# Mamba-like mixer, block-sparse layer and attention on one core: the last mixer tile and the layer norm behind it in another order

## The chip, the core and the metric

One NeuronCore of one Trainium2 chip. Its engines are TensorE (PE in the profile; PEld is its weight load), VectorE (DVE), ScalarE (ACT), GpSimd (POOL) and SyncE (SP), which issues the transfers. Each engine takes its instructions in the order in which they are written; they meet through semaphores (`then_inc`, `wait_ge`). Matmul results land in PSUM, eight banks of 128 x 512 f32. The metric is the device time of one execution in microseconds, as the median of several.

## What is computed

1024 tokens (4 sequences of 256) of width 512 pass four residual layers. Cut to what matters here:

```python
x = x + mixer(layernorm(x))        # 128 heads of 64, chunks of 128 tokens
x = x + blocksparse(layernorm(x))  # the second layer norm; the change reaches to here
x = x + attention(layernorm(x))
x = x + gated_dense(layernorm(x))

# mixer, per head: decay within and between chunks
Lmat = exp(segment_sum(A*dt));  M = (C @ B.T) * Lmat
Y = M @ (x*dt) + between_chunks;  y = Y + D*x
y = y * rsqrt(mean(y*y) + eps) * norm_w * silu(gate)
out = y @ out_proj_w.T             # 8192 -> 512

# blocksparse: in each block of 32 of 1792 features, only the largest counts
inter = xf @ c1_w.T @ c2_w.T
idx = argmax(inter.reshape(.., 56, 32), -1)
h = relu(w1[idx] . xf);  out = sum(h * w2t[idx])
```

## The kernel before

Everything is kept transposed: features on the 128 partitions, tokens along the row. The mixer's 8192 inner features are 64 tiles `t` of 128 (two heads each), in 8 groups of 8. A list written out by hand for each engine is the order of the work; nothing is scheduled at run time. Products that need f32 accuracy are split into three fast ones (`split`, L583 to L585: high by high, low by high, high by low).

One slot of the mixer handles tile `t` and prepares tile `t + 1`. TensorE projects the next tile's x part into banks 0, 1 (`XB`) and its gate into banks 2, 3 (`GB`); it transposes tile `t` (`turn`, L617, into `YB`, banks 6, 7), it multiplies finished tiles by the output weights (`out_part`, 12 matmuls of 512 columns a call, into XB and then GB, added up by VectorE's `out_sum`, L1571), and it does the mixing itself (`outputs`, L637 and L641, into YB). ScalarE makes three decay tiles a slot: `fall_of(t, k, 0)` and `fall_of(t, k, 1)` (eight activations L1113, then an exponential L1117) and `exp_of` (L1124). All three lie in banks 4, 5 (`LB`), so each waits until VectorE has read the one before (`weigh`, L1563 for the first two, L1565 for the third). `turned` (L1556) takes the transposed tile, `outputs` needs it and all three `weigh`. Then VectorE forms y and z (L1631, L1635; for the last tile in halves of 512 tokens, L1655, L1658). ScalarE rounds z (`z_high`, L1135), GpSimd forms its low part (`z_low`, L439).

The last slot, t = 63, has no next tile. TensorE turns the tile and then does both output parts for tiles 60 and 61, and `outputs`.

Behind the groups stand, in this order: the root mean square of y (`f0` sums L729, `last_root` L1264, `last_inverse` L1667, spread to all partitions by L530); eight output parts of the last two tiles (`last_part(n)`, 6 matmuls each; n < 4 for the first 512 tokens, the rest for the second), each followed on VectorE by an add L1673 and a multiplication L1678 and on GpSimd by the addition to x (L481).

The second layer norm is done in two halves h of 512 tokens: `mean` (PE L523 on x), copy (ACT L1077), `mean_wide` (PE L530), `center` (DVE L1463), `square` (ACT L1081), `spread` (PE L523 on sq), `root` (ACT L1085), `inverse` (DVE L1468), `spread_wide` (PE L530), `scaled` (DVE L1472). Then comes the choice of blocks: `c1_part` (PE L747, f32 matmuls of 512 columns, four k for each half), `t1_high` (ACT L1268), `t1_sum` (DVE L1684), and a loop of 16 steps v: `in_part` (PE L759), reduce and compare (DVE L1719, L1723), `turn_part` (PE L796), `turned_part` (ACT L1288), `first_part` (PE L807), `mask_part` (ACT L1294). The step's compare is two behind the `in_part` it lets go. `first_part` writes the bank in which `c1_part` of half 1 lies, so the first of them waits for `t1_sum(1)`. Before the last step TensorE does the first hidden tile of the sparse layer (`hidden(0)`, L583 to L585). When the last mask is there, VectorE makes the first hidden activation (L1733), and TensorE is busy with the sparse layer from there on.

## Time and profile before

| | us |
|---|---|
| three runs | 2156.98, 2158.49, 2161.08 |
| median | 2158.49 |
| the profiled execution | 2162.24 |
| its span, first to last instruction | 2160.4 |
| TensorE busy | 2074.7 (96%) |
| VectorE busy | 1582.5 (73%) |
| ScalarE busy | 1439.5 (67%) |
| GpSimd busy | 759.0 (35%) |
| mean granted TensorE clock | 0.988 of full speed |

Busy time is a sum over all stages. The chain of work that ended last is 90% TensorE. The profile's picture of 40 slices shows TensorE at nine tenths or more nearly everywhere but in slices 26 to 28, the stretch from about 1430 to 1540 us. The change lies in that stretch.

### The profile page before, as it was taken

To read this page: it belongs to the slowest core of one execution; us is meant where nothing else is said; L and a number is where in the kernel's file an instruction comes from. 1 tells how busy PE (TensorE), PEld (TensorE's weight loads), DVE (VectorE), ACT (ScalarE), POOL (GpSimd) and SP (SyncE) were. 2 spreads that over 40 slices of the span, in tenths; PEclk is the share of its full clock that TensorE was granted. 3 is DMA by queue.
4 is the path that set the end of the run, shared out by engine and by line. 5 is a ranking of instruction groups with operands and counts; after the bars stand their busy time and mean duration, and the time that the engine had idled before them with its cause. 6 is when DMAs were issued, how large, how long until landed. Compare 5 with 4: busy or idle time off the path is not lost.

```text
span 2160.4 us, 33511 instructions
## 1 busy us (share of the span) xinstructions
PE 2074.7 (96%) x12936; PEld 1665.1 (77%) x12940; DVE 1582.5 (73%) x1701; ACT 1439.5 (67%) x3108; POOL 759.0 (35%) x391
## 2 busy tenths in 40 slices
PE   6899999999999999999999999986899989999998
PEld 4788888888888888888888888874677677777764
DVE  6778788778878887878887887777433357777765
ACT  4777786777777777777677677773533357777761
POOL 2244454444454345444444445433444100000001
PEclk9999999999999999999999999998999989999999
DMA  2222222221222122222222222221222010000001
GB/s 104 108 88 87 80 108 78 77 100 69 98 83 104 69 98 88 76 91 108 70 77 104 73 98 78 98 69 31 90 90 96 20 40 17 24 18 17 18 3 39
DMA packets 49341, 155.84 MB, mean 72 GB/s; under 512 B 13856, under 2 KB 20256, under 8 KB 40736
## 3 DMA queue, kind: packets, MB, share of 16 engines
q1 hardware_dynamic: 49184, 153.70, 20.5%
q8 instruction: 104, 1.70, 0.3%
q14 instruction: 53, 0.43, 0.1%
HBM read 151.06 MB, written 2.62 MB: 71 GB/s over the span
## 4 chain that ended last, share of the span: by engine, by line
PE 90%; DVE 7%; ACT 2%; issue 1%; DMA 0%; SPq 0%; DVEq 0%; ACTq 0%
PE PS L583 20%; PE PS L585 19%; PE PS L584 19%; PE PS L641 6%; PE PS L824 4%; PE PS L948 3%; PE PS L617 3%; PE PS L637 3%; PE PS L932 2%; PE PS L577 2%; PE PS L919 2%; PE PS L955 2%; PE PS L921 1%; PE PS L920 1%; DVE arena L1533 1%
## 5 line engine op out<-in xcount | busy, mean ns | idle before, releaser
L583 PE MATMUL PS<-xnh,wh 128*128 128x512 f32 x1272 | 510.3, 401 | 8.9 <-DVE xnl L1496 6.1
L585 PE MATMUL PS<-xnh,wl 128*128 128x512 f32 x1272 | 497.4, 391 | 0.0
L584 PE MATMUL PS<-xnl,wh 128*128 128x512 f32 x1272 | 496.5, 390 | 0.0
L1533 DVE SCALAR_TENSOR_TENSOR arena<-PS,arena 128x1020 f32<-128x1020 f32 (+2 forms) x240 | 305.6, 1273 | 31.2 <-ACT arena L1152 25.5
L1113 ACT ACTIVATE PS<-x,arena 128x128 f32<-128x128 f32 x1024 | 307.9, 354 | 22.6 <-DVE arena L1565 20.2
L583 PEld LDWEIGHTS PS<-xnh,wh 128*128 128x128 f32 x1272 | 239.6, 188 | 63.7 <-issue 14.7
L439 POOL TENSOR_TENSOR zl<-arena,zh 128x1024 fp32r<-128x1024 f32 x63 | 176.4, 2800 | 295.1 <-ACT zh L1135 295.1
L585 PEld LDWEIGHTS PS<-xnh,wl 128*128 128x128 f32 x1272 | 239.3, 188 | 52.1
L584 PEld LDWEIGHTS PS<-xnl,wh 128*128 128x128 f32 x1272 | 240.0, 189 | 46.1
L435 POOL TENSOR_TENSOR arena<-arena 128x1024 f32<-128x1024 f32 x63 | 152.0, 2412 | 296.7 <-ACT arena L1131 296.7
L424 POOL TENSOR_TENSOR wl<-arena,wh 128x1024 fp32r<-128x1024 f32 x72 | 174.8, 2428 | 200.3 <-ACT wh L1105 200.3
L583 PE MATMUL PS<-zh,woh 128*128 128x512 f32 x496 | 194.1, 391 | 0.0
L584 PE MATMUL PS<-zl,woh 128*128 128x512 f32 x496 | 194.1, 391 | 0.0
L585 PE MATMUL PS<-zh,wol 128*128 128x512 f32 x496 | 194.0, 391 | 0.0
L1571 DVE TENSOR_TENSOR sq<-sq,PS 128x1024 f32<-128x1024 f32 x124 | 150.7, 1220 | 43.3 <-PE PS L585 43.1
L641 PE MATMUL PS<-arena 128*64 128x128 f32 x2048 | 170.9, 277 | 4.4 <-DVE arena L1565 4.4
L1556 DVE TENSOR_TENSOR arena<-PS,arena 128x1024 f32<-128x1024 f32 x64 | 78.4, 1225 | 132.1 <-PE PS L617 132.1
L1765 DVE TENSOR_REDUCE arena<-PS 128x2 f32<-128x512 f32 x128 | 88.6, 693 | 113.4 <-PE PS L921 112.2
L1148 ACT ACTIVATE arena<-PS 128x1024 f32<-128x1024 f32 x64 | 65.7, 1027 | 148.6 <-PE PS L585 148.6
L1563 DVE TENSOR_TENSOR arena<-PS,arena 128x1024 f32<-128x1024 f32 x128 | 156.1, 1219 | 3.7 <-ACT PS L1117 1.5
L1124 ACT ACTIVATE PS<-x,arena 128x128 f32<-128x128 f32 x512 | 153.8, 357 | 2.2 <-DVE arena L1563 2.2
L641 PEld LDWEIGHTS PS<-arena 128*64 128x64 f32 x2048 | 120.6, 137 | 27.1 <-issue 27.1
(237 smaller groups left out, 4132.9 us busy)
## 6 DMA issues: line engine op xcount, KB each, us to landing
x<-decay SPq DMA_DIRECT2D x64, 1024.0 KB, 4.6
arena<-in_w_xg SPq DMA_DIRECT2D x72, 512.0 KB, 5.5
arena<-in_w_o SPq DMA_DIRECT2D x32, 512.0 KB, 3.4
arena<-in_w_f SPq DMA_DIRECT2D x28, 512.0 KB, 3.4
arena<-in_w_h SPq DMA_DIRECT2D x16, 257.0 KB
x<-in_x SPq DMA_DIRECT2D x3, 1024.0 KB, 7.4
out<-x SPq DMA_DIRECT2D x8, 256.0 KB, 2.0
x<-in_x SPq DMA_DIRECT2D x2, 512.0 KB, 4.2
```

Of the source, the lines that this page charges most:

```text
L424: nc.gpsimd.tensor_tensor(wl[:, k], w_raw, wh[:, k].bitcast(F32), ALU.subtract).then_inc(s["wlo"], 1)
L435: nc.gpsimd.tensor_tensor(sumsq, sumsq, ysq, ALU.add).then_inc(s["ssq"], 1)
L439: nc.gpsimd.tensor_tensor(zl[:, k], zt[:, k], zh[:, k].bitcast(F32), ALU.subtract).then_inc(s["zlo"], 1)
L583: mm(PS[:, bank], ah, bh, start=(n == 0), stop=False)
L584: mm(PS[:, bank], ah, bl, start=False, stop=False)
L585: last = mm(PS[:, bank], al, bh, start=False, stop=(n == len(terms) - 1))
L641: last = mm(PS[H, YB + u // 4, col(u % 4)], xdt[:, u, H], ring[:, hh, col(u)], start=(u % 2 == 0), stop=True)
L1113: last = act(PS[:, LB + u // 4, col(u % 4)], rowB[:, 2 * k + hh, col(u)], ACT.Relu, scale=-1.0, bias=aT[:, u, 2 * t + hh:2 * t + hh + 1])
L1124: last = act(PS[:, LB + b // 2, col(2 * hh + b % 2)], rowB[:, 2 * k + hh, col(2 * b + 1)], ACT.Exp, bias=fromend[:, k, b, hh:hh + 1])
L1533: ins = stt(o, pair_of(bank).rearrange("p q (b t) -> p q b t", t=SEQ)[:, :, :, :SEQ - k], w[:, 3 - k:4 - k], o, ALU.mult, ALU.add)
L1563: tt(both(ring[:, hh]), pair_of(LB), both(by[:, 0:TOK]), ALU.mult).then_inc(s["used"], 1)
L1571: tt(both(sq[:, m]), both(sq[:, m]), pair_of(bank), ALU.add).then_inc(s["oacc"], 1)
```

## The change

It has three parts. In the last mixer slot TensorE does one output part ahead of the turn, into GB, and the second decay tile is written to XB instead of LB. The other output part goes to XB when VectorE has read that decay tile. `outputs` signals after each half of the tokens, y of the first half waits for the first signal only, and `last_y`/`last_z` are two functions with `last_low` between them. Behind it, only `last_part(0)` stands ahead of the spread of the root mean square, where two stood. In the second layer norm the mean and centring of half 1 come directly behind those of half 0, the rest of half 1 before the choice of blocks rather than within its first steps, and `c1_part` of half 1 ends in step 0 rather than in step 1.

```diff
                     for hh in range(2):
                         last = mm(PS[H, YB + u // 4, col(u % 4)], xdt[:, u, H], ring[:, hh, col(u)], ...)
+                    if t == NT - 1 and u == NU // 2 - 1:
+                        last.then_inc(s["Y_ps"], 1)
                 last.then_inc(s["Y_ps"], 1)
+            def last_slot(t, k, q):
+                pe.wait_ge(s["oacc"], 2 * t - 4)
+                pe.wait_ge(s["wolo"], q + 1)
+                pe.wait_ge(s["zlo"], 2 * q + 3)
+                out_part(2 * k, GB)
+                turn(t, k)
+                pe.wait_ge(s["used"], 3 * t + 3)
+                out_part(2 * k + 1, XB)
+                outputs(t)
...
             last_part(0)
-            last_part(1)
             pe.wait_ge(s["f0_rc"], 2)
             pe.wait_ge(s["yv"], NT + 2)
...
-            for n in range(2, 7):
+            for n in range(1, 7):
                 last_part(n)
...
             mean_wide(1, 0)
-            spread(1, 0)
             pe.wait_ge(s["x1"], 2 * KD)
             mean(1, 1)
+            mean_wide(1, 1)
+            spread(1, 0)
             spread_wide(1, 0)
-            mean_wide(1, 1)
+            spread(1, 1)
             pe.wait_ge(s["f_in"], 16 * 4)
             pe.wait_ge(s["ln_xn"], 3)
-            c1_part(0, A, range(KD))
+            c1_part(0, A, range(2))
+            spread_wide(1, 1)
+            c1_part(0, A, range(2, KD))
             in_part(0)
-            spread(1, 1)
             in_part(1)
-            spread_wide(1, 1)
             pe.wait_ge(s["ln_xn"], 4)
+            c1_part(1, Y0, range(2))
...
-                if v < 2:
-                    c1_part(1, Y0, range(2 * v, 2 * v + 2))
+                if v == 0:
+                    c1_part(1, Y0, range(2, KD))
@@ ScalarE
                     if final and i == TPG - 1:
-                        fall_of(t, k, 1)
+                        fall_of(t, k, 1, XB)
+                        exp_of(t, k, freed=2)
                         squares(t - 1)
                         wo_high(NT // 2 - 1, woh_last)
-                        exp_of(t, k)
...
             mean(1, 0, 0)
+            mean(1, 1, 4)
             square(1, 0)
             root(1, 0, 0)
-            mean(1, 1, 4)
             square(1, 1)
+            root(1, 1, 4)
             t1_high(0, A)
-            root(1, 1, 4)
...
-                if v == 1:
+                if v == 0:
                     t1_high(1, Y0)
@@ VectorE
+                    if final and i == TPG - 1:
+                        weigh(t, 1, XB)
+                        turned(t)
+                        weigh(t, 2)
+                        out_sum(2 * k, GB, 2 * t - 3)
+                        out_sum(2 * k + 1, XB, 2 * t - 2)
+                        continue
...
-            for h in range(2):
-                last_y(h)
+            last_y(0)
+            last_z(0)
+            last_y(1)
             last_low(0)
+            last_z(1)
             last_inverse(0)
+            last_inverse(1)
             last_low(1)
-            last_inverse(1)
...
             center(1, 0)
+            center(1, 1)
...
             inverse(1, 0)
             scaled(1, 0)
-            center(1, 1)
+            inverse(1, 1)
+            scaled(1, 1)
             t1_sum(0, A)
...
-                if v == 1:
-                    inverse(1, 1)
-                    scaled(1, 1)
-                if v == 3:
+                if v == 2:
                     t1_sum(1, Y0)
```

How instructions stand on the engines. ScalarE in the last slot, before (L1113 and L1117 are a decay tile in LB, L1131 the squares, L1161 the output weights, L1124 `exp_of`):

```order
783 L1113 ACTIVATE PS<-x,arena 128x128 x8
784 L1117 ACTIVATE PS<-PS 128x1024
785 L1131 ACTIVATE arena<-arena 128x1024
786 L1161 ACTIVATE wh<-arena 128x1024
787 L1124 ACTIVATE PS<-x,arena 128x128 x8
788 L1174 ACT_TABLE_LOAD
```

and of the changed kernel, where the same functions have the lines L1126, L1130, L1144, L1174 and L1137:

```order
783 L1126 ACTIVATE PS<-x,arena 128x128 x8
784 L1130 ACTIVATE PS<-PS 128x1024
785 L1137 ACTIVATE PS<-x,arena 128x128 x8
786 L1144 ACTIVATE arena<-arena 128x1024
787 L1174 ACTIVATE wh<-arena 128x1024
788 L1187 ACT_TABLE_LOAD
```

`exp_of` has moved ahead of the squares and of the output weights.

VectorE in the last slot, before (L1556 `turned`, L1563 and L1565 `weigh`, L1571 `out_sum`, L1655 y and L1658 z in halves):

```order
914 L1556 TENSOR_TENSOR arena<-PS,arena 128x1024
915 L1563 TENSOR_TENSOR arena<-PS,arena 128x1024
916 L1571 TENSOR_TENSOR sq<-sq,PS 128x1024
917 L1565 TENSOR_TENSOR arena<-PS,arena 128x1024
918 L1571 TENSOR_TENSOR sq<-sq,PS 128x1024
919 L1655 SCALAR_TENSOR_TENSOR arena<-arena,PS 128x512
920 L1658 SCALAR_TENSOR_TENSOR arena<-arena 128x512
```

and of the changed kernel (`turned` L1569, `weigh` L1576 and L1578, `out_sum` L1584, y L1673, z L1678):

```order
914 L1576 TENSOR_TENSOR arena<-PS,arena 128x1024
915 L1569 TENSOR_TENSOR arena<-PS,arena 128x1024
916 L1578 TENSOR_TENSOR arena<-PS,arena 128x1024
917 L1584 TENSOR_TENSOR sq<-sq,PS 128x1024 x2
918 L1673 SCALAR_TENSOR_TENSOR arena<-arena,PS 128x512
919 L1678 SCALAR_TENSOR_TENSOR arena<-arena 128x512
```

The second `weigh` has moved ahead of `turned`, and both output sums behind the third `weigh`.

TensorE in the second layer norm and the first steps of the choice of blocks, before (L530 a spread to all partitions, L523 a sum on x or on its squares sq, L747 `c1_part`, L759 `in_part`, L796 `turn_part`):

```order
5682 L530 MATMUL PS<-arena,cst 128x128 x4
5683 L523 MATMUL PS<-sq,cst 32x128 x16
5684 L523 MATMUL PS<-x,cst 32x128 x16
5685 L530 MATMUL PS<-arena,cst 128x128 x8
5686 L747 MATMUL PS<-arena 128x512 x4
5687 L759 MATMUL PS<-zl,zh 128x448 x2
5688 L523 MATMUL PS<-sq,cst 32x128 x16
5689 L759 MATMUL PS<-zl,zh 128x448 x2
5690 L530 MATMUL PS<-arena,cst 128x128 x4
5691 L796 MATMUL PS<-identB,arena 128x128 x7
5692 L759 MATMUL PS<-zl,zh 128x448 x2
5693 L747 MATMUL PS<-arena 128x512 x2
```

and of the changed kernel (L756 is `c1_part`, L768 `in_part`, L806 `turn_part`):

```order
5682 L530 MATMUL PS<-arena,cst 128x128 x4
5683 L523 MATMUL PS<-x,cst 32x128 x16
5684 L530 MATMUL PS<-arena,cst 128x128 x4
5685 L523 MATMUL PS<-sq,cst 32x128 x16
5686 L530 MATMUL PS<-arena,cst 128x128 x4
5687 L523 MATMUL PS<-sq,cst 32x128 x16
5688 L756 MATMUL PS<-arena 128x512 x2
5689 L530 MATMUL PS<-arena,cst 128x128 x4
5690 L756 MATMUL PS<-arena 128x512 x2
5691 L768 MATMUL PS<-zl,zh 128x448 x4
5692 L756 MATMUL PS<-arena 128x512 x2
5693 L806 MATMUL PS<-identB,arena 128x128 x7
```

The mean of half 1 (on x) has moved ahead of the squares of half 0, the squares and both spreads of half 1 ahead of `in_part`, and the first half of the second `c1_part` ahead of the first `turn_part`.

## Rows read from the trace of the kernel before

**Rows 1.** Busy time by stage: us, engines' busy times, TensorE clock, DMA share, GB/s.

```profile
0.00:1431.00 1431.00, 1403.53 (x8785) 1167.16 (x8786) 1151.13 (x927) 1047.90 (x2109) 627.17 (x298) 1.00 0.25 88
1431.00:1451.00 20.00, 15.29 (x136) 12.86 (x135) 14.54 (x14) 14.63 (x33) 7.16 (x3) 0.91 0.32 107
1451.00:1468.00 17.00, 14.81 (x136) 11.19 (x136) 14.61 (x23) 3.00 (x7) 8.96 (x7) 1.00 0.00 1
1468.00:1501.00 33.00, 19.61 (x166) 11.17 (x162) 19.99 (x25) 7.86 (x9) 8.92 (x5) 0.84 0.25 50
1501.00:1529.00 28.00, 19.10 (x138) 11.51 (x141) 27.35 (x27) 26.32 (x32) 13.56 (x6) 0.94 0.07 20
...
1539.00:2160.00 621.00, 595.05 (x3548) 445.94 (x3548) 353.11 (x688) 334.48 (x915) 92.78 (x72) 0.98 0.13 39
```

**Rows 2.** Timeline, TensorE, last slot: start, duration, instruction, [idle before, releaser].

```profile
1438.66 1.94 PE L617 MATMUL PS<-cst,arena 128*128 128x128 f32 x8 [3.09 <-DVE arena L1631]
...
1446.98 0.44 PE L641 MATMUL PS<-arena 128*64 128x128 f32 x4 [0.43 <-DVE arena L1565]
```

**Rows 3.** Timeline, VectorE, last slot.

```profile
1440.71 1.23 DVE L1556 TENSOR_TENSOR arena<-PS,arena 128x1024 f32<-128x1024 f32 x1 [0.87 <-PE PS L617]
...
1445.61 1.23 DVE L1565 TENSOR_TENSOR arena<-PS,arena 128x1024 f32<-128x1024 f32 x1 [0.52 <-ACT PS L1124]
...
1449.86 0.75 DVE L1655 SCALAR_TENSOR_TENSOR arena<-arena,PS 128x512 f32<-128x512 f32 x1 [1.90 <-PE PS L641]
```

**Rows 4.** Timeline, ScalarE, last slot.

```profile
1437.36 2.42 ACT L1113 ACTIVATE PS<-x,arena 128x128 f32<-128x128 f32 x8 [1.36 <-DVE arena L1563]
...
1443.16 2.42 ACT L1124 ACTIVATE PS<-x,arena 128x128 f32<-128x128 f32 x8 [0.43 <-DVE arena L1563]
```

**Rows 5.** Timeline, GpSimd, slots of tiles 61 and 63, and the last addition to x.

```profile
1413.68 3.49 POOL L439 TENSOR_TENSOR zl<-arena,zh 128x1024 fp32r<-128x1024 f32 x1 [11.40 <-ACT zh L1135]
...
1448.12 2.37 POOL L439 TENSOR_TENSOR zl<-arena,zh 128x1024 fp32r<-128x1024 f32 x1 [1.47 <-ACT zh L1135]
...
1468.46 1.27 POOL L481 TENSOR_TENSOR x<-x,sq 128x512 f32<-128x512 f32 x1 [1.03 <-DVE sq L1678]
```

**Rows 6.** Timeline, VectorE, beside the first row of rows 5.

```profile
1416.64 1.61 DVE L1635 SCALAR_TENSOR_TENSOR arena<-arena 128x1024 f32<-128x1024 f32 x1
```

**Rows 7.** Timeline, TensorE, from the last output parts to step 1.

```profile
1453.70 0.47 PE L583 MATMUL PS<-zh,wh 128*128 128x512 f32 x1 [0.23 <-DVE zl L1663]
...
1456.59 0.73 PE L530 MATMUL PS<-arena,cst 1*128 1x128 f32 x16
...
1464.27 1.08 PE L523 MATMUL PS<-x,cst 128*32 128x128 f32 x32
...
1472.58 1.93 PE L523 MATMUL PS<-sq,cst 128*32 128x128 f32 x32 [4.36 <-ACT sq L1081]
...
1478.99 5.37 PE L747 MATMUL PS<-arena 128*128 128x512 f32 x8 [2.08 <-DVE arena L1472]
1486.00 0.65 PE L759 MATMUL PS<-zl,zh 128*128 128x448 f32 x2 [1.64 <-DVE zh L1684]
...
1497.78 1.88 PE L747 MATMUL PS<-arena 128*128 128x512 f32 x4
```

**Rows 8.** Timeline, VectorE, layer norm to step 3, and the first hidden activation.

```profile
1468.30 2.28 DVE L1463 TENSOR_TENSOR arena<-x,PS 128x2048 f32<-128x2048 f32 x1
...
1476.55 2.29 DVE L1472 TENSOR_TENSOR arena<-arena,PS 128x2048 f32<-128x2048 f32 x1 [0.62 <-PE PS L530]
...
1500.99 1.08 DVE L1719 TENSOR_REDUCE arena<-PS 128x28 f32<-128x896 f32 x1
...
1537.38 0.63 DVE L1733 SCALAR_TENSOR_TENSOR arena<-PS,arena 128x512 f32<-128x512 f32 x1
```

**Rows 9.** One line, the reduce of the loop: shortest, median, longest ns, first and last start.

```profile
L1719 DVE TENSOR_REDUCE arena<-PS x16: 1080/1082/1096, 1486.7 to 1526.6; 128x28 f32<-128x896 f32 x16
```

**Rows 10.** Timeline, ScalarE, the squares of half 0.

```profile
1470.61 1.91 ACT L1081 ACTIVATE sq<-arena 128x2048 f32<-128x2048 f32 x1 [4.92 <-DVE arena L1463]
```

More of the change, by code:

```diff
@@ L648, in group @@
                     n = None if final and i == TPG - 1 else t + 1
+                    if n is None:
+                        last_slot(t, k, PPG * g + i // 2 - 1)
+                        continue
                     outs = not (first and i < 2)
@@ L685, in group @@
                         q = PPG * g + i // 2 - 1
-                        if n is not None:
-                            pe.wait_ge(s["conv_x"], t + 2)
-                        else:
-                            pe.wait_ge(s["oacc"], 2 * t - 5)
+                        pe.wait_ge(s["conv_x"], t + 2)
                         pe.wait_ge(s["wolo"], q + 1)
@@ L692, in group @@
                         out_part(2 * k, XB)
-                        if n is not None:
-                            pe.wait_ge(s["sgd"], t + 2)
-                        else:
-                            pe.wait_ge(s["oacc"], 2 * t - 4)
+                        pe.wait_ge(s["sgd"], t + 2)
                         out_part(2 * k + 1, GB)
@@ L738, in last_part @@
                 if n < KD:
-                    pe.wait_ge(s["oacc"], 2 * (NT - 2) - (n < 2))
+                    pe.wait_ge(s["oacc"], 2 * (NT - 2))
                 else:
@@ L1105, in high, with fall_of @@
                 act(wh[:, k], w_raw, ACT.Copy).then_inc(s["whi"], 1)
-            def fall_of(t, k, hh):
+            def fall_of(t, k, hh, bank=LB):
                 if hh == 0:
                     ac.wait_ge(s[f"rows{k}"], 16 * (t // 2) + 16)
-                ac.wait_ge(s["used"], 3 * t + hh + 1)
-                L = pair_of(LB)
+                if bank == LB:
+                    ac.wait_ge(s["used"], 3 * t + hh + 1)
+                else:
+                    ac.wait_ge(s["oacc"], 2 * t - 5)
+                L = pair_of(bank)
                 for u in range(NU):
-                    last = act(PS[:, LB + u // 4, col(u % 4)], rowB[:, 2 * k + hh, col(u)], ACT.Relu, scale=-1.0,
+                    last = act(PS[:, bank + u // 4, col(u % 4)], rowB[:, 2 * k + hh, col(u)], ACT.Relu, scale=-1.0,
                                bias=aT[:, u, 2 * t + hh:2 * t + hh + 1])
@@ L1117, in fall_of, with exp_of @@
                 act(L, L, ACT.Exp, scale=-1.0).then_inc(s["exps"], 1)
-            def exp_of(t, k):
+            def exp_of(t, k, freed=3):
                 ac.wait_ge(s["fromend"], t + 1)
-                ac.wait_ge(s["used"], 3 * t + 3)
+                ac.wait_ge(s["used"], 3 * t + freed)
                 for b in range(NB):
@@ L1557, in turned, with weigh @@
                    across(dtT[:, :, bass.ds(2 * t, 2)].unsqueeze(3), (P, NU, 2, HP)), ALU.mult).then_inc(s["xdt"], 1)
-            def weigh(t, hh):
+            def weigh(t, hh, bank=LB):
                 ve.wait_ge(s["exps"], 3 * t + hh + 1)
@@ L1562, in weigh @@
                 if hh < 2:
-                    tt(both(ring[:, hh]), pair_of(LB), both(by[:, 0:TOK]), ALU.mult).then_inc(s["used"], 1)
+                    tt(both(ring[:, hh]), pair_of(bank), both(by[:, 0:TOK]), ALU.mult).then_inc(s["used"], 1)
                 else:
@@ L1589, in group @@
                         ve.wait_ge(s["gtm"], 2 * g + 2)
-                    if not (final and i == TPG - 1):
-                        weigh(t, 0)
+                    if final and i == TPG - 1:
[4 more added lines that the diff above has]
+                        out_sum(2 * k + 1, XB, 2 * t - 2)
+                        continue
+                    weigh(t, 0)
                     if side == 1:
@@ L1625, in group @@
                     ve.wait_ge(s["Y_ps"], t + 1)
-                    if final and i == TPG - 1:
-                        continue
                     if final and i == TPG - 2:
@@ L1653, in last_y, with last_z @@
             def last_y(h):
+                ve.wait_ge(s["Y_ps"], NT + h)
                 ve.wait_ge(s["sqd"], NT)
                 stt(yt[:, half(h)], xs[:, 1, half(h)], prm[:, NT - 1, 5:6], PS[:, YB + h], ALU.mult, ALU.add).then_inc(s["yv"], 1)
+            def last_z(h):
                 ve.wait_ge(s["yv"], NT + 1 + h)
```

## The prediction

> **What bounds the kernel now.** I read the time by stage first, then the timeline of each engine in the stretch that the change touches, following the releaser in brackets from engine to engine. By stage [rows 1], TensorE is busy 1403.5 of the first 1431 us and 595 of the last 621: there it is the bound, and the change leaves both alone. Between 1431 and 1539 us it is not: 15.3 of 20 us, 14.8 of 17, 19.6 of 33, 19.1 of 28. What bounds these 108 us is a chain that hops between engines, and the reader is to see it in four pieces.
>
> In the last slot TensorE stands idle 3.09 us until VectorE has formed y of tile 62 (L1631), and then runs its eight transposes in 1.94 us [rows 2]. ScalarE's second decay tile waits 1.36 us for the first `weigh`, and `exp_of` starts only at 1443.16 [rows 4]. So the third `weigh`, which releases `outputs`, starts at 1445.61 [rows 3] and `outputs` at 1446.98 [rows 2]; y starts when all of it is there, at 1449.86 [rows 3]. The first output part waits for z's low part, at 1453.70 [rows 7].
>
> From there to the last addition to x, TensorE's parts are the bound, one after another (14.8 us busy of 17). In the layer norm each step waits for the one before; `in_part(0)` starts at 1486.00 [rows 7]. In the choice of blocks VectorE needs two instructions a step: step 3's reduce starts at 1500.99 [rows 8] and the last, step 15's, at 1526.6 [rows 9], 2.13 us a step, and VectorE is busy 27.35 of 28 us [rows 1]. From `in_part(0)` to step 3 it takes 15.0 us, since half 1 of the norm and its `c1_part` stand in between.
>
> **The change, part by part.** I play the chain forward with durations of the rows and hand-over gaps of about 0.1 us as they show.
>
> *Last slot.* Tile 62's slot ends as before. The first output part needs the sums of slot 62, which are there, and fills TensorE's 3.09 us of idle time: 12 matmuls. Their pace is from rows 7: between 1457.25, the end of the spread at 1456.59 less its tail, and 1464.27 stand five parts, 7.0 us, so 1.36 to 1.4 a part of 6 and 2.7 for 12. The turn can't be earlier than 1438.66, since L1631 hasn't moved, but it follows work directly. ScalarE goes from its first exponential (the second decay tile waited 1.36 from 1436.0) straight to XB: 2.42 + 1.02 gives 1439.45, then `exp_of` 2.42 to 1441.9, which was 1443.16 + 2.42 = 1445.6: 3.7 earlier. On VectorE, z of tile 62 ends at 1439.8; behind it `weigh` to XB to 1441.0, `turned` to 1442.15, the third `weigh` to 1443.3 (1.2 each, rows 3). TensorE's second output part has to wait for the first of these, an added wait: 1441.15 to 1443.9, and `outputs` stands behind it in the queue. So `outputs` starts at 1443.9 instead of 1446.98, 3.1 us earlier. If TensorE finds itself at the low clock there, part and outputs take up to 1.7 longer.
>
> *Ahead of the output parts.* `outputs` takes 2.8 us and signals at its half, 1445.35; the two sums (2.4 from 1443.3) end at 1445.6, and y of half 0 follows: 4.3 us earlier than 1449.86. That would bring the first part to about 1449.2. But another releaser comes last now. GpSimd has three instructions to do, 2.4 us each: squares, output weights' low part, z's low part of tile 62. The first waits for ScalarE's squares, which stand behind `exp_of` now and are no earlier than before, so the third ends near 1450.1 instead of 1450.5, and the first output part can't start before it. Beside VectorE's L1635, which reads two operands from SBUF, that third instruction took 3.49 us and L1635 1.61, against 2.37 where it had little beside it [rows 5, 6]; now VectorE's z and low part of z, of the same kind, lie beside it, so I add 1.1: 1451.3. The price is between 0 (1450.2) and 1.1 with this row; I take the latter. The spread needs two inverses, done by 1451.2, and follows the first part at 1452.7 instead of 1456.59: 3.9 earlier. Behind it stand seven parts instead of six, 1.4 more: 2.5 left at the end of part 7.
>
> The Trainium skill, "GPSIMD Engine Reference", section 8, says that GpSimd shares its SBUF interfaces with VectorE, with contention for VectorE instructions that have two SBUF inputs. By that rule the earlier z slows GpSimd here; rows 5 and 6 agree with it (3.49 against 2.37). Without it the sum would be 1.1 larger.
>
> *Layer norm, half 0.* Centring starts at 1465.9 instead of 1468.30 [rows 8]: 2.4 gained. ScalarE has the mean copy of half 1 ahead of the squares of half 0 now. It waits for the last addition to x (1468.46 + 1.27 [rows 5], less 2.4: 1467.3), 1.1 of sums and 0.3 of copy: the squares start at 1468.8, where they could have started at 1468.2. Against 1470.61 [rows 10] that leaves 1.8. The squares' sum, root, inverse (behind centring of half 1 and 1.4 us of small VectorE instructions), spread and scaling keep 1.8: `scaled` at 1474.7 instead of 1476.55 [rows 8], and `c1_part` at 1477.1 instead of 1478.99 [rows 7].
>
> *c1 and the clock.* Its eight instructions took 5.37 us, where four of the next, in 1497.78's row, took 1.88: full clock would be 3.5 to 3.8, and 5.37 is the first half at half speed. The granted clock averages 0.84 in that stage [rows 1], since TensorE idles between the steps: 4.36 us ahead of 1472.58, whose row took 1.93 against 1.08 for the same shape at 1464.27. I take the same low clock for the first half, as TensorE's work ahead of it is still thin; the spread of half 1 (0.5) now stands within it. c1 is done at 1482.8 instead of 1484.36, and `in_part(0)` at 1484.4 instead of 1486.00: **1.6 gained** so far.
>
> *Steps 0 to 3.* Two steps of 2.13 on VectorE end at 1489.4. TensorE does two `in_part`s (0.9), half of `c1_part(1)` (1.8), turn and `in_part` (0.9, after compare 0 at 1487.3), and its second half (1.8): 1489.9. `t1_high` 0.6, `t1_sum` 0.75 bring 1491.4 for step 2 and 1493.5 for step 3, against 1500.99. That is 9.1 us from `in_part(0)`, instead of 15.0: **5.9 gained**, the largest term. It is VectorE's inverse and scaling of half 1 (3.2) with their waits, and `c1_part(1)` cut in two by steps 0 and 1, where its second half started only at 1497.78 [rows 7].
>
> *The loop and its end.* Twelve steps at 2.13 are the same. The first hidden activation comes 8.6 us after the last compare (1526.6 + 2.2 to 1537.38), because ScalarE's masks lag: it is busy 26.3 of 28 us [rows 1]. It now starts its masks about 2 us earlier relative to VectorE, of which VectorE's pace takes most back; I count **0.5**. Later stages move as a block.
>
> Sum: 1.6 + 5.9 + 0.5 = 8.0 us. The profiled execution of 2162.24 would be 2154.2; the median of the runs stands 3.75 below it, so 2158.49 - 8.0 = **2150.5**.
>
> **The rivals.**
> - *The clock stays full through `c1_part`.* TensorE has less idle time ahead of it. For: the mean of half 1 now lies in the long gap. Against: two gaps of over 1.5 us remain. It gives 1.6 more, 2148.9; with GpSimd's 1.1 as well, 2147.8.
> - *The clock is low for longer,* through both `c1_part`s. For: the stage averages 0.84 now. The second half of c1(0) and both of c1(1) at half speed cost 1.8 each, less 0.7 that was so before: 4.7, leaving 3.3 and 2155.2. This is no measurable change: a measurement of this kernel can tell about 0.2%, 4.3 us.
> - *ScalarE's mask queue, not VectorE, sets the loop's end.* The first mask follows `t1_sum` of half 1, which moves from about 1501.0 (the start of step 3's reduce) to 1491.4; all of it would reach the end: 9.6 gained, 2148.9. For: 26.3 of 28 us busy, and 8.6 us of tail. Against: its remaining 1.7 us of idle time and VectorE's 27.35.
> - *Slower.* TensorE's work in the last slot is now cut by new waits (1439.7 to 1441.15, and 1446.8 to 1451.3), and the clock falls for the output parts behind them, which are the bound of their stage: 8 parts of 1.36 double, 10.9, and the sums of the norm with c1 low too, 4.7 and 1.5. 8.0 - 17.1 = -9.1: 2167.6. It decides from about 16 us of bound TensorE work at half speed on. Against: the clock was 1.00 in 1451 to 1468 [rows 1], behind waits of the same kind.
>
> The Trainium skill, "TensorE: Matmul & The Clock Gate", Part 1, says that the throttled state is the default and activity releases it. The trace agrees (1.93 after 4.36 idle, 1.08 after work); by it alone both clock rivals are open, and none of the sums uses it.
>
> **Chances.** Forecast 0.60 (2150.5, own range 2149 to 2152.5), full clock 0.15, mask queue 0.08, clock low for longer 0.11, slower 0.04; 0.02 for anything else. The range leaves out the slower case and the outer ends of the clock cases: 2147.3 to 2154.8. Faster by over 0.2% (below 2154.2): 0.85; within: 0.11; slower: 0.04.
>
> **What would show it.** Right: an output part directly ahead of the turn, and the turn near 1.0 us; `outputs` near 1443.9; GpSimd as the releaser of the first output part, near 1451; `in_part(0)` near 1484.4; no inverse or scaling between steps 0 and 1; step 3's reduce near 1493.5; the first hidden activation near 1529.4. Wrong: the squares of half 0 later than 1469.5, a `c1_part` of half 1 at half speed, ScalarE unbroken from step 1 on, or a stage behind 1539 that grows.

## The result, and the profile after

| | before | after |
|---|---|---|
| median of 20 runs each, us | 2160.72 (2156.98 to 2166.81) | 2156.98 (2150.86 to 2161.24) |
| profiled execution, us | 2162.24 | 2154.79 |
| its span, us | 2160.4 | 2153.0 |

After to before is 0.9982, 95% interval 0.9974 to 0.9989: by this ratio the change gains 3.9 us (2.4 to 5.6), half of the 8.0 forecast; the two medians differ by 3.7. The time stands above the range's upper end of 2154.8. The two profiled executions differ by 7.4 us, but not all of it is the change's. That the profiled execution of after, at 2154.79, lies near the 2154.2 of the prediction is luck. The stretch in question begins with y of tile 62 on VectorE, and that instruction starts 2.75 us apart although nothing ahead of it was changed. Timeline, VectorE, of before (start, duration, instruction):

```profile
1437.24 1.27 DVE L1631 SCALAR_TENSOR_TENSOR arena<-arena,PS 128x1024 f32<-128x1024 f32 x1
```

The same view after:

```profile
1434.49 1.27 DVE L1648 SCALAR_TENSOR_TENSOR arena<-arena,PS 128x1024 f32<-128x1024 f32 x1
...
1442.96 0.75 DVE L1673 SCALAR_TENSOR_TENSOR arena<-arena,PS 128x512 f32<-128x512 f32 x1
1443.74 1.52 DVE L1678 SCALAR_TENSOR_TENSOR arena<-arena 128x512 f32<-128x512 f32 x1
...
1446.02 2.01 DVE L1683 TENSOR_TENSOR zl<-arena,zh 128x512 fp32r<-128x512 f32 x1
1447.95 0.74 DVE L1678 SCALAR_TENSOR_TENSOR arena<-arena 128x512 f32<-128x512 f32 x1
...
1450.58 0.63 DVE L1683 TENSOR_TENSOR zl<-arena,zh 128x512 fp32r<-128x512 f32 x1
...
1495.80 1.08 DVE L1740 TENSOR_REDUCE arena<-PS 128x28 f32<-128x896 f32 x1
...
1531.42 0.63 DVE L1754 SCALAR_TENSOR_TENSOR arena<-PS,arena 128x512 f32<-128x512 f32 x1
```

So I count from this instruction's start in every trace. To the first hidden activation it is 100.14 us before (1537.38 in [rows 8]) and 96.93 after: 3.2 us. The rest of the 7.4 lies outside. One profile is one execution, though: e8 below, which is after with nine matmuls more and has after's median, needs 100.31 for the same stretch in its profile. So a distance within one profile says where time went in that execution, and what a change is worth is read from the medians and ratios.

By stage after (us, busy times of TensorE, weight load, VectorE, ScalarE, GpSimd, TensorE clock, DMA share, GB/s), to hold against [rows 1]:

```profile
1431.00:1451.00 20.00, 15.65 (x152) 11.98 (x148) 18.63 (x18) 15.26 (x34) 7.50 (x3) 0.92 0.23 81
1451.00:1468.00 17.00, 14.26 (x134) 10.81 (x133) 13.08 (x18) 0.62 (x3) 12.24 (x10) 0.90 0.00 1
1468.00:1501.00 33.00, 25.32 (x158) 13.56 (x159) 22.69 (x27) 11.49 (x14) 5.64 (x2) 0.69 0.26 50
```

The third row is the one to stop at: the same 33 us, about as many TensorE instructions (158 against 166), and TensorE busy 25.3 us instead of 19.6. It has hardly more work; its granted clock fell from 0.84 to 0.69. TensorE's timeline says which instructions paid. First the last slot, where the change did as meant:

```profile
1435.91 1.06 PE L617 MATMUL PS<-cst,arena 128*128 128x128 f32 x8 [0.16 <-DVE arena L1648]
1438.40 0.50 PE L583 MATMUL PS<-zh,woh 128*128 128x512 f32 x1 [1.42 <-DVE arena L1576]
...
1441.38 0.44 PE L641 MATMUL PS<-arena 128*64 128x128 f32 x4
...
1448.29 0.77 PE L583 MATMUL PS<-zh,wh 128*128 128x512 f32 x1 [0.94 <-DVE zl L1683]
1448.85 0.63 PE L584 MATMUL PS<-zl,wh 128*128 128x512 f32 x1
...
1452.11 0.40 PE L584 MATMUL PS<-zl,wh 128*128 128x512 f32 x1
```

The turn follows work and takes 1.06 us, not 1.94 [rows 2]. The first output part (from 1448.29) ran at 0.63 us a matmul and the next at 0.40: it began at the low level of the clock. Matmuls overlap, so their starts tell the pace: 0.43 us apart at 0.63, 0.23 apart at 0.39. Then the layer norm and c1, the same view:

```profile
1463.59 0.51 PE L530 MATMUL PS<-arena,cst 1*128 1x128 f32 x8 [0.78 <-DVE sq L1693]
1465.65 1.93 PE L523 MATMUL PS<-x,cst 128*32 128x128 f32 x32 [1.56 <-POOL x L481]
1467.98 0.81 PE L530 MATMUL PS<-arena,cst 1*128 1x128 f32 x8 [0.40 <-ACT arena L1087]
1469.78 1.93 PE L523 MATMUL PS<-sq,cst 128*32 128x128 f32 x32 [0.98 <-ACT sq L1091]
1473.48 0.81 PE L530 MATMUL PS<-arena,cst 1*128 1x128 f32 x8 [1.77 <-DVE arena L1481]
...
1476.80 3.75 PE L756 MATMUL PS<-arena 128*128 128x512 f32 x4 [0.64 <-DVE arena L1485]
1480.47 0.81 PE L530 MATMUL PS<-arena,cst 1*128 1x128 f32 x8
1481.22 3.78 PE L756 MATMUL PS<-arena 128*128 128x512 f32 x4
1486.64 1.05 PE L768 MATMUL PS<-zl,zh 128*128 128x448 f32 x4 [1.64 <-DVE zh L1704]
1487.53 1.88 PE L756 MATMUL PS<-arena 128*128 128x512 f32 x4
```

Four c1 matmuls take 3.75 and 3.78 us here and 1.88 in the last row; the 32 small sums take 1.93 where the same shape took 1.08 in [rows 7]. From the sum at 1465.65 to the end of `c1_part(0)` everything runs at the low level, 1.2 GHz (the granted clock of that stretch is 0.50, in the last section). Before, the eight matmuls of `c1_part(0)` took 5.37 together [rows 7]; now 7.5.

One table holds the whole case, in us from the start of y of tile 62. "Forecast" is the prediction's times less 1437.24; e1, e2, e3 and e10 are the experiments below.

| start of | before | forecast | after | e1 | e2 | e3 | e10 |
|---|---|---|---|---|---|---|---|
| first half y | 12.62 | 8.4 | 8.47 | 8.45 | 12.07 | 8.47 | 12.39 |
| centring of half 0 | 31.06 | 28.7 | 29.68 | 31.73 | 30.53 | 29.35 | 32.44 |
| `scaled` of half 0 | 39.31 | 37.5 | 39.87 | 39.98 | 39.58 | 38.10 | 41.19 |
| `t1_sum(0)` | 47.86 | | 51.26 | 48.34 | 50.96 | 45.59 | 48.67 |
| reduce of step 3 | 63.75 | 56.3 | 61.31 | 64.10 | 63.62 | 55.64 | 58.72 |
| first hidden activation | 100.14 | 92.2 | 96.93 | 100.55 | 100.85 | 91.75 | 94.82 |

### The profile page after: what moved, and what is told of

It reads as the page before. It is cut to its first block, busy times and chain, and to the rows that moved or that the text cites. A ratio compares the mean times of both kernels' runs of the same rounds, so it can differ in the third digit from the quotient of the medians.

```text
span 2153.0 us, 33511 instructions
## 1 busy us (share of the span) xinstructions
PE 2075.0 (96%) x12936; PEld 1663.3 (77%) x12940; DVE 1584.8 (74%) x1701; ACT 1438.7 (67%) x3108; POOL 759.6 (35%) x391
## 4 chain that ended last, share of the span: by engine, by line
PE 90%; DVE 7%; ACT 1%; issue 1%; DMA 0%; POOL 0%; SPq 0%; DVEq 0%; ACTq 0%
PE PS L583 20%; PE PS L585 19%; PE PS L584 19%; PE PS L641 6%; PE PS L834 4%; PE PS L958 3%; PE PS L617 3%; PE PS L637 3%; PE PS L942 2%; PE PS L577 2%; PE PS L929 2%; PE PS L965 2%; PE PS L931 1%; PE PS L930 1%; DVE arena L1546 1%
## 5 line engine op out<-in xcount | busy, mean ns | idle before, releaser
L1126 ACT ACTIVATE PS<-x,arena 128x128 f32<-128x128 f32 x1024 | 307.9, 355 | 21.1 <-DVE arena L1578 20.1
L1584 DVE TENSOR_TENSOR sq<-sq,PS 128x1024 f32<-128x1024 f32 x124 | 150.6, 1220 | 42.2 <-PE PS L585 42.1
L1569 DVE TENSOR_TENSOR arena<-PS,arena 128x1024 f32<-128x1024 f32 x64 | 78.3, 1224 | 131.0 <-PE PS L617 131.0
L1161 ACT ACTIVATE arena<-PS 128x1024 f32<-128x1024 f32 x64 | 65.7, 1027 | 148.6 <-PE PS L585 148.6
L1576 DVE TENSOR_TENSOR arena<-PS,arena 128x1024 f32<-128x1024 f32 x128 | 156.1, 1220 | 3.7 <-ACT PS L1130 1.6
L1137 ACT ACTIVATE PS<-x,arena 128x128 f32<-128x128 f32 x512 | 153.9, 358 | 1.5 <-DVE arena L1576 1.5
```

Source lines behind the costliest of these rows:

```text
L1126: last = act(PS[:, bank + u // 4, col(u % 4)], rowB[:, 2 * k + hh, col(u)], ACT.Relu, scale=-1.0, bias=aT[:, u, 2 * t + hh:2 * t + hh + 1])
L1137: last = act(PS[:, LB + b // 2, col(2 * hh + b % 2)], rowB[:, 2 * k + hh, col(2 * b + 1)], ACT.Exp, bias=fromend[:, k, b, hh:hh + 1])
L1576: tt(both(ring[:, hh]), pair_of(bank), both(by[:, 0:TOK]), ALU.mult).then_inc(s["used"], 1)
L1584: tt(both(sq[:, m]), both(sq[:, m]), pair_of(bank), ALU.add).then_inc(s["oacc"], 1)
```

## Experiments

The theory after the result: the clock, low from the norm's sums through both halves of `c1_part(0)`, eats half of the gain. Rivals: the slot's new waits or contention between VectorE and GpSimd eat it; or the norm's new order costs its half 0 more than thought. All times are against the kernel before on the same chip, as a ratio with its 95% interval.

**e1_slot_only: the new slot, the norm as before.**

```
             mean_wide(1, 0)
+            spread(1, 0)
             pe.wait_ge(s["x1"], 2 * KD)
...
-            c1_part(0, A, range(2))
-            spread_wide(1, 1)
-            c1_part(0, A, range(2, KD))
+            c1_part(0, A, range(KD))
             in_part(0)
+            spread(1, 1)
```
(cut; the rest of TensorE's order up to step 1, and ScalarE's and VectorE's, are put back likewise)

> The last slot, the half-wise signal and the one part ahead of the spread as in the changed kernel; the layer norm and the choice of blocks as before. In the changed kernel's profile, set against y of tile 62, the first mean_wide of the norm comes 1.4 us earlier than before. Clock theory (the slot's gain is real, and TensorE's low clock in the norm and in c1_part ate the rest of the forecast): 1 to 2.5 us faster than before, ratio 0.9989 to 0.9995. Rival (the new order of the norm brings nothing, the slot is the whole gain): 3.9 us, ratio 0.9982.

Measured: 2160.88 us, 0.9998 (0.9989 to 1.0007). A miss: no gain at all from a slot whose first half y starts 4.2 us earlier. TensorE's timeline shows the output parts:

```profile
1448.80 0.47 PE L583 MATMUL PS<-zh,wh 128*128 128x512 f32 x1 [0.94 <-DVE zl L1681]
...
1451.23 1.24 PE L530 MATMUL PS<-arena,cst 1*128 1x128 f32 x16 [0.31 <-DVE arena L1685]
...
1453.84 0.63 PE L583 MATMUL PS<-zh,wh 128*128 128x512 f32 x1
```

Eleven matmuls, nearly two parts' worth, ran at 0.63 or more instead of 0.39, where the parts are the bound, and centring starts at 31.73 instead of 31.06 although the first output sum starts 1.7 earlier (16.64 against 18.38). In this execution the clock fell behind the slot's waits, the place of the slower rival. That the slot's waits are the cause isn't shown: e10 below has the old slot, and eight of its output matmuls were low too.

**e2_norm_only: the slot as before, the norm's new order.** The kernel before with the changed kernel's order in the norm and the choice of blocks, on all three engines, among it these lines:

```
-            c1_part(0, A, range(KD))
+            c1_part(0, A, range(2))
+            spread_wide(1, 1)
+            c1_part(0, A, range(2, KD))
             in_part(0)
...
             scaled(1, 0)
-            center(1, 1)
+            inverse(1, 1)
+            scaled(1, 1)
             t1_sum(0, A)
```

> The last slot and the output parts as before; the norm and c1_part in the new order. Clock theory: steps 0 to 3 are 5.9 us shorter, both halves of c1_part(0) run at half speed as in the changed kernel's profile and cost 3 to 4: 2 to 3 us faster than before, ratio 0.9986 to 0.9991. Rival (the order brings nothing): ratio 1.000. If the clock falls only because of what the new slot does ahead of it, this kernel gains more than the changed one, 5 us, ratio 0.9977.

Measured: 2157.73 us, 0.9987 (0.9978 to 0.9996): a gain of 2.8, as expected by the clock theory. Its TensorE timeline has the same slow c1:

```profile
1478.27 3.75 PE L747 MATMUL PS<-arena 128*128 128x512 f32 x4 [0.56 <-DVE arena L1474]
...
1482.69 3.78 PE L747 MATMUL PS<-arena 128*128 128x512 f32 x4
...
1489.74 3.62 PE L747 MATMUL PS<-arena 128*128 128x512 f32 x4
```

In this execution even the first half of `c1_part(1)` is slow (3.62), and the profile shows no gain left at the hidden activation (100.85). So the long low stretch comes with the norm's new order, slot or no slot: in all four profiles with that order and no fillers in the norm (after, e2, e5, e8) the halves of `c1_part(0)` took 3.75 and 3.78, in the three with the old order (before, e1, e4) 5.18 to 5.40 together. Its end moves from execution to execution.

**e3_fill: the changed kernel with matmuls that nobody reads, in TensorE's gaps.**

```
+            def fill(n, bank):
+                for _ in range(n):
+                    mm(PS[:, bank], woh[:, 0, 0:P], wol[:, 0], start=True, stop=True)
...
+            pe.wait_ge(s["oacc"], 2 * (NT - 2))
+            fill(1, E)
             for h in range(2):
...
+                fill(4, E)
...
             mean_wide(1, 0)
+            pe.wait_ge(s["ol_m"], 2 * KD)
+            fill(4, S)
...
+            pe.wait_ge(s["ln_xc"], 3)
+            fill(3, E)
             spread(1, 0)
+            fill(5, E)
             spread_wide(1, 0)
             spread(1, 1)
+            fill(2, S)
...
             c1_part(0, A, range(2, KD))
+            pe.wait_ge(s["ln_xn"], 4)
+            fill(4, S)
             in_part(0)
```

> The changed kernel, with matmuls of 512 columns whose result nothing reads, put into TensorE's waits from the last outputs to in_part(0) (1, 4 and 4 beside the f0 sums; 4, 3, 5, 2 and 4 in the norm). Clock theory: the clock stays full, both halves of c1_part(0) take 1.9 instead of 3.75 us, the three sums of the norm 1.1 instead of 1.9: 4 to 6 us faster than the changed kernel, 8 to 10 faster than before, ratio 0.9955 to 0.9965. Rival (hand-overs and ScalarE's order, not the clock, ate the gain): as the changed kernel, ratio 0.998; a filler that delays the next real matmul would show as 0.5 us slower.

Measured: 2151.82 us, 0.9961 (0.9949 to 0.9973): 8.4 us faster than before, with 27 matmuls more than the changed kernel. TensorE's timeline, norm and c1 (L735 is the filler):

```profile
1466.93 1.08 PE L523 MATMUL PS<-x,cst 128*32 128x128 f32 x32 [0.18 <-POOL x L481]
...
1470.21 1.08 PE L523 MATMUL PS<-sq,cst 128*32 128x128 f32 x32 [0.39 <-ACT sq L1106]
1471.22 1.42 PE L735 MATMUL PS<-wol,woh 128*128 128x512 f32 x5
...
1476.61 1.95 PE L763 MATMUL PS<-arena 128*128 128x512 f32 x4 [0.83 <-DVE arena L1500]
1478.49 0.50 PE L530 MATMUL PS<-arena,cst 1*128 1x128 f32 x8
1478.92 1.98 PE L763 MATMUL PS<-arena 128*128 128x512 f32 x4
```

Each row of the changed kernel's own work is here at the other level: 1.08 for 1.93, 1.95 for 3.75, 0.50 for 0.81. The first hidden activation comes at 91.75, 5.2 us earlier than after. From centring to `t1_sum(0)` it is 16.2 us here and 21.6 after; this distance is used again below.

**e7_fill_norm and e8_fill_parts: only the fillers from `mean_wide(1, 0)` on; only those beside the first output sums.** Each keeps one part of e3's edit.

> The changed kernel with the unread matmuls in the norm only (4, 3, 5, 2, 4). Clock theory with the loss in the norm and c1_part: most of the 4.5 us between the changed kernel and the filled one, ratio to before 0.996 to 0.9968. If the low clock in the output parts is half of the loss: 0.997.

> The changed kernel with the unread matmuls beside the f0 sums only (1, 4, 4). Clock theory with the loss in the norm: as the changed kernel, 0.998, the first output parts at full clock; 0.5 to 1 us better if the parts' low clock reached the end.

Measured: e7 2150.35 us, 0.9956 (0.9943 to 0.9969); e8 2156.76 us, 0.9983 (0.9974 to 0.9992). The gain is in the norm's fillers; those beside the first output sums add nothing that these runs can tell. The profiled execution of e7, at 2155.20 the slowest of its five, had 17 output matmuls at the low level and reached centring only at 32.56, but from there to `t1_sum(0)` it too took 16.2 us. The granted clock of one stretch in three kernels shows why (one row each: e3, e7, e8):

```profile
1465.00:1487.00 22.00, 18.34 (x173) 10.52 (x174) 16.85 (x21) 6.10 (x7) 8.94 (x5) 1.00 0.39 75
```

```profile
1465.00:1487.00 22.00, 17.77 (x182) 10.42 (x171) 15.67 (x21) 5.49 (x7) 11.08 (x7) 1.00 0.38 76
```

```profile
1465.00:1487.00 22.00, 16.07 (x136) 8.33 (x136) 12.74 (x17) 5.02 (x6) 8.91 (x5) 0.54 0.37 75
```

The changed kernel has 0.54 there, like e8.

**e9_fill_narrow: e3 with fillers of 32 columns instead of 512.** Same places, same added waits, same number of instructions.

```
-                    mm(PS[:, bank], woh[:, 0, 0:P], wol[:, 0], start=True, stop=True)
+                    mm(PS[:, bank, 0:32], woh[:, 0, 0:P], wol[:, 0, 0:32], start=True, stop=True)
```

> The filled kernel with the same number of unread matmuls at the same places, with the same waits, but of 32 columns instead of 512. If it is the clock that the filling holds up (work on TensorE, not the added instructions or waits): the clock falls again, both halves of c1_part(0) take 3.75 us, and the time is that of the changed kernel, ratio to before 0.998. If the gain came from the added waits or another side effect of the edit: 0.996, as with 512 columns.

Measured: 2155.55 us, 0.9984 (0.9975 to 0.9992), the changed kernel's ratio. TensorE's timeline:

```profile
1472.39 1.93 PE L523 MATMUL PS<-sq,cst 128*32 128x128 f32 x32 [0.54 <-ACT sq L1106]
...
1479.11 3.01 PE L763 MATMUL PS<-arena 128*128 128x512 f32 x4
...
1482.48 1.98 PE L763 MATMUL PS<-arena 128*128 128x512 f32 x4
```

The sums of squares and most of the first c1 half are slow, the second half is fast. By the ratios (intervals 0.9949 to 0.9973 and 0.9975 to 0.9992) what e3 gains it gains by TensorE's work, not by the waits or by the instructions being there. In this one profile narrow fillers hold the clock in part: from centring to `t1_sum(0)` it is 17.6 us, nearer to e3's 16.2 than to the 21.6 of after, and twelve output matmuls ahead of it were low.

**e10_norm_only_fill: e2 with the norm's fillers**, as in e7.

> The norm's new order on the kernel before, with the unread matmuls of 512 columns in the norm. With the changed kernel filled in the same places (0.9956) it shows what the new last slot is worth once the clock is no longer between: if the slot is worth the 1.6 us by which the first output sum comes earlier, this one has 0.9964; if the slot is worth nothing, 0.9956. Norm order alone had 0.9987, so the clock theory expects 4.5 to 5.5 us below that.

Measured: 2152.09 us, 0.9969 (0.9958 to 0.9980); c1 at 1.95 and 1.98. Against e2 (0.9987) the fillers are worth 0.0018 or 3.9 us, somewhat less than the 4.5 expected at least; on the whole change they are worth 5.6 (e7 against after). Against e7 (0.9956) the slot's share is 0.0013, 2.8 us, but the two intervals overlap. The interval holds the 0.9964 expected with a slot worth 1.6 us, and just leaves out the 0.9956 of a slot worth nothing.

**e4_before_fill: fillers in the kernel before.** If the clock alone made the difference, before would gain too.

```
+            pe.wait_ge(s["oacc"], 2 * (NT - 2))
+            fill(5, E)
             for h in range(2):
...
+                fill(3 * (1 - h), E)
...
             mean_wide(1, 0)
+            pe.wait_ge(s["ol_m"], 2 * KD)
+            fill(14, S)
             spread(1, 0)
...
             c1_part(0, A, range(KD))
+            fill(4, B)
```

> The kernel before, with such matmuls in its waits (5 and 3 beside the f0 sums, 14 ahead of the squares' sum of half 0, 4 behind c1_part(0)). Clock theory: there the low clock cost the first half of c1_part(0) 1.7 us, the sums 1.5 and the first part of c1_part(1) 0.9, of which 2 to 3 us lie on the chain: ratio 0.9986 to 0.9991. Rival: no change, 1.000.

Measured: 2158.61 us, 0.9999 (0.9991 to 1.0008): a miss, no gain. The sum of squares is fast, but c1 is not:

```profile
1470.32 1.08 PE L523 MATMUL PS<-sq,cst 128*32 128x128 f32 x32 [0.68 <-ACT sq L1091]
...
1476.42 5.40 PE L754 MATMUL PS<-arena 128*128 128x512 f32 x8 [2.82 <-DMA arena<-in_c]
...
1491.29 3.31 PE L754 MATMUL PS<-arena 128*128 128x512 f32 x4
```

The fillers stand ahead of the spread; behind them is a wait of 2.82 us (for `scaled`, which ends at 1475.74, then for a DMA), and c1 then takes the 5.40 that it took before (5.37 in [rows 7]), with the first half of `c1_part(1)` slow as well (3.31; it took 2.78 before). The kernel before was not filled where it mattered, so this run does not say what it would be worth with a full clock, and no other run does. How much of the fillers' gain the old order could have had stays open.

**e5_early_weights: the last output weights are split one slot earlier**, on ScalarE (`wo_high`) and GpSimd (`wo_low`), so that GpSimd has two instructions left behind the last slot, not three.

```
-                    if final and i == TPG - 1:
+                    if final and i == TPG - 2:
                         wo_low(NT // 2 - 1, wol_last, woh_last)
+                    if final and i == TPG - 1:
                         z_low(t - 1, 0)
```

> The changed kernel, with the last output weights rounded by ScalarE and their low part taken by GpSimd one slot earlier (GpSimd idles 17 us there), so that GpSimd's low part of z for tile 62 is done by about 3.5 us sooner and hardly lies beside VectorE's z and low part of z. Contention theory (these two took 1.52 and 2.01 us instead of 0.75 and 0.69 because GpSimd read SBUF beside them): both near their old durations, the first sum of an output part starts 14.9 instead of 16.8 us after y of tile 62, and the whole 1 to 2 us faster than the changed kernel if the clock behind it allows, ratio to before 0.997 to 0.9982. Rival (the order of half 0 and 1 on VectorE is what delays them): durations stay, ratio 0.9982.

Measured: 2155.78 us, 0.9983 (0.9973 to 0.9993), no different from after. VectorE's timeline:

```profile
1445.77 1.81 DVE L1680 SCALAR_TENSOR_TENSOR arena<-arena 128x512 f32<-128x512 f32 x1
...
1448.34 0.69 DVE L1685 TENSOR_TENSOR zl<-arena,zh 128x512 fp32r<-128x512 f32 x1
```

The low part of z, 2.01 after, is 0.69 with GpSimd idle beside it; z, 1.52 after, is 1.81, since GpSimd's z_low (1444.65 to 1447.03) now lies beside it, which I had not counted on. The first output sum starts at 15.60 instead of 16.80, where 14.9 was expected. These 1.2 us of chain aren't seen in the time: the ratios are 0.9983 and 0.9982. The slow c1 stays (3.75, 3.78).

**e6_fill_early: e3 and e5 together**, with `fill(4 - 2 * h, E)` beside the first output sums.

> The same together with the unread matmuls in TensorE's waits (2 instead of 4 behind the second f0 sum). If clock and contention are two separate losses they add: 1.5 to 2 us faster than with the unread matmuls alone (ratio 0.9961), ratio 0.995 to 0.9956. If the contention is hidden behind the GpSimd additions to x, 0.996.

Measured: 2150.09 us, 0.9953 (0.9941 to 0.9965), the lowest ratio of all: 10.2 us below before and clear of the changed kernel's interval. It isn't told apart from e3 or e7. Whether e5's 1.2 us adds to the fillers' gain stays open. In the profiles e6 is 1.1 us ahead of e3 at centring (28.27 against 29.35), but only 0.2 at the first hidden activation (91.51 against 91.75), since in e6 the clock was low again for the sum on x of half 1 (1.54) and the squares' sum of half 0 (1.94), although full-width fillers stood beside them.

## Why the prediction was wrong, step by step

The forecast played the chain forward, and most links came out as written. One did not, TensorE's clock, and by the start of `in_part(0)` it had cost 5 us.

*The slot.* Right in the profile. `outputs` starts 6.89 after y of tile 62, before 9.74 [rows 2]: 2.85 earlier where 3.1 stood. The first half y starts at 8.47; 8.4 stood. No part of the change failed to do what it says.

*The first output part.* Right in time by luck, wrong in cause. It starts at 13.80 (14.06 forecast). I named GpSimd as last releaser, its third instruction stretched by 1.1; the row says `DVE zl L1683`. GpSimd's z_low went only from 2.37 [rows 5] to 2.81, and ended at 1447.48. It was VectorE that paid: 1.52 for z, which takes 0.74 at 1447.95 with GpSimd done, and 2.01 for the low part that takes 0.63 at 1450.58 with GpSimd idle. The two stretches, 0.8 and 1.3, happen to make up for the releaser that I misnamed. e5 shows that it is GpSimd beside them. GpSimd's timeline after, to hold against VectorE's above:

```profile
1442.34 2.38 POOL L443 TENSOR_TENSOR wl<-arena,wh 128x1024 fp32r<-128x1024 f32 x1
1444.67 2.81 POOL L439 TENSOR_TENSOR zl<-arena,zh 128x1024 fp32r<-128x1024 f32 x1
```

In these rows the one that starts second is the one that is stretched, as if it waited for the other to finish. z starts within L443 and ends 0.54 after it (alone it takes 0.75); z_low starts within z and ends 2.22 after it (alone 2.37); the low part starts within z_low and ends 0.55 after it (alone 0.63 to 0.69). [rows 5] and [rows 6] fit this too, and I had misread them: z_low's 3.49 started together with another VectorE instruction with operands in SBUF (L1543, 1413.68, its usual 1.22), while L1635, which I had named, lay beside its last 0.5 us only and was stretched itself. So the forecast's 1.1 us on GpSimd would have needed a VectorE instruction that starts first.

The Trainium skill, "GPSIMD Engine Reference", section 8, names contention with VectorE instructions that have two SBUF inputs; the rows agree, and L1673, whose second operand is in PSUM, stays at 0.75.

*Centring.* 1.4 earlier where 2.4 stood. The missing 1.0 is the first output part at the low clock: from its start to the spread behind it are 2.83 us, where the forecast had 1.4; its start, 0.3 ahead of the forecast, gives a part of this back.

*Squares and `scaled` of half 0.* Forecast 1.8 earlier, measured 0.0 for the squares (33.34 us against 33.37 [rows 10]) and 0.6 later for `scaled`. The mean of half 1, which the change puts ahead, took 1.93 and not 1.08, its spread 0.81 and not 0.50: the price of a step that is put in front of the chain doubled with the clock.

*c1 and the clock: the step that failed.* The prediction said "I take the same low clock for the first half, as TensorE's work ahead of it is still thin". c1 done at 45.6, `in_part(0)` at 47.2, 1.6 gained. Measured: both halves slow, 3.75 and 3.78, with the spread between them at 0.81; `in_part(0)` at 52.15, 3.4 us later than before. That is 5.0 us against the forecast, and hardly any of it comes back behind it: 5.05 at step 3, 4.8 at the first hidden activation. Of the 5.0, 1.0 had come in by centring, 0.8 more by the squares, 0.6 more by `scaled`, and 2.5 in c1 itself, which the forecast put at 5.7 us with its spread and which took 8.2. I judged the clock by how much work lies ahead of c1. What the trace shows is many small steps with gaps of 0.6 to 1.8 us, in which the work itself is stretched by the low clock; TensorE is then busy in 25.3 of 33 us and still not at full clock.

The prediction had this outcome as its rival "the clock is low for longer", with a gain of 3.3 us, and gave it 0.11. The gain came out as 3.9 by the ratio and 3.2 in the two profiles. Its mechanism was close, but that its price fits is partly luck: it had both halves of `c1_part(1)` slow, which were fast in the profile of after (in those of e2 and e8 the first took 3.62), and it had nothing for the norm's sums and the first output part. Nor was 3.3 us "no measurable change": the interval of 2.4 to 5.6 us leaves out zero. That it is the clock, e3, e7 and e9 show: with the same order, full-width fillers give 0.9961 and 0.9956, narrow ones with e3's waits 0.9984; e10 against e2 points the same way. With the clock held, the rest of the sum comes out as well: for a full clock the prediction had 9.6 us, and e3 and e7 gain 8.4 and 9.5. [rows 1] already had 0.84 in that stage and [rows 7] a 5.37; the right reading was that a new order of small steps there leaves the clock open to both sides, and that the low side was the one already seen.

The Trainium skill, "TensorE: Matmul & The Clock Gate", Part 1, says that the throttled state is the default and activity releases it. I cited it and let it change nothing. The rows agree with it: 1.93 in the sums of after, 1.08 once fillers stand between them.

*Steps 0 to 3.* Right: 9.16 us from `in_part(0)` to step 3's reduce, 9.1 forecast, 14.99 before, so 5.8 gained and 5.9 forecast. No inverse or scaling stands between the steps, and `c1_part(1)` is whole at 1.88.

*The loop and its end.* 35.6 us from step 3's reduce to the first hidden activation, before 36.4: 0.8 gained, 0.5 forecast. ScalarE's queue does set the end, as the rival had it. Its timeline and TensorE's after (L1307 is `mask_part`, L1301 `turned_part`, L817 `first_part`):

```profile
1523.77 0.92 ACT L1307 ACTIVATE arena<-PS 128x896 bf16<-128x896 f32 x1
1526.95 0.92 ACT L1301 ACTIVATE arena<-PS 128x896 bf16<-128x896 bf16 x1 [2.26 <-PE PS L806]
```

```profile
1523.20 0.54 PE L817 MATMUL PS<-arena 128*128 128x512 bf16 x2 [1.20 <-ACT arena L1307]
```

From 1498.53 to 1524.69 ScalarE has no idle time; `first_part` waits for a mask within that stretch, `hidden(0)` follows it, and ScalarE then waits for the turn behind `hidden(0)`. In all twelve profiles the first hidden activation starts 6.7 us after the end of this stretch, but 7.9 to 8.8 after VectorE's last compare. The stretch ends 3.2 us earlier than before, as the activation does; VectorE's last reduce is 2.6 earlier. What failed of the rival is its price: `t1_sum` of half 1 is 4.6 us earlier, and 3.2 of that reach the end.

*The slower rival* did not come. The low output parts that it named are seen in five profiles: after (6 matmuls), e1 (11), e7 (17), e9 (12) and e10 (8), the last with the old slot. They are absent in before, e2 and e5, and in all four with full-width fillers beside the first sums (e3, e4, e6, e8).

*The anchor.* The three runs shown had a median of 2158.49, all 20 with them 2160.72. Of the 6.5 us between the forecast and the result, 2.2 come from this and 4.3 from the gain.

*What stays open.* Why the clock falls where it does in one execution and not in another. After and e2 have the same waits ahead of the mean of half 1 (0.78 and 1.56 us); that mean took 1.93 in the one and 1.08 in the other. So e1's 0.9998 and the slot's 0.0013 in e10 against e7 both stand, and what the slot is worth lies between nothing and about 3 us. I have not separated these further.

## What to carry to other kernels

Before you shorten a chain of small TensorE steps, mark every matmul on it that the profile shows at either level of the clock, and price the new order with all of them slow and with all of them fast; if the two sums differ by more than the gain, the clock is the case. Where small steps can't be packed, full-width matmuls into an idle bank in their gaps are a cheap way to test it, and here they were worth 4.5 to 5.6 us beside the 3.9 that the reordering had brought; e6 shows that they don't hold the clock in every execution. When you name an engine as last releaser because another stretches it, ask which of the two is stretched: look which starts first.

## What the runs showed of the hardware

- VectorE instructions that read two SBUF operands were stretched two to three times when they started within a GpSimd instruction (0.75 to 1.52 or 1.81; 0.69 to 2.01), and GpSimd's when it started within or with one of VectorE's (2.37 to 2.81 after, 3.49 in [rows 5]). Each time the second ended 0.1 to 0.2 us less than its own usual duration after the first: the rows look like taking turns, not like sharing. VectorE's with one PSUM operand kept their 0.75.
- A row at the low clock is not far from double for wide matmuls (3.75 against 1.95 for four of 512 columns in f32; 1.93 against 1.08 for 32 small sums), and less for tiny ones (0.81 against 0.50 for eight spreads).
- TensorE stayed at the low clock for 19 us (1465.65 to 1485) in after, while busy 15.06 of 19.5 us. Between the last row at full level (1463.59) and the first low one lie waits of 0.78 and 1.56 us; the longest wait within the low stretch was 1.77. From 1465 to 1487 the granted clock was 0.54 in after, 1.00 with fillers of 512 columns in e3, e7 and e10, but 0.84 in e6 with the same fillers, and 0.77 with those of 32 columns in e9. The rows of that view, changed kernel first, then e9:

```profile
1465.00:1484.50 19.50, 15.06 (x128) 8.05 (x128) 11.22 (x15) 4.61 (x5) 8.23 (x5) 0.50 0.44 85
```

```profile
1465.00:1487.00 22.00, 18.00 (x165) 11.87 (x164) 14.46 (x20) 5.24 (x7) 10.34 (x7) 0.77 0.38 76
```
